# Attention in six float32 groups a unit: small float32 products moved next to the larger ones

## The reference

```python
q = xt @ Wq.T                                  # xt: x of a batch, turned; 8 heads of 32
scores = scale * einsum('bhqd,bhkd->bhqk', qh, qh)
logits = (scores * cmask + (1.0 - cmask) * NEG) * rmask
attn = softmax(logits, axis=-1)
ctx = einsum('bhqk,bhkd->bhqd', attn, qh)
out = ctx @ Wo.T                               # turned back, then the expert layers with a top-2 router
```

## Time and profile before

| what | us |
|---|---|
| median of 3 runs (1988.9 to 1992.98) | 1990.24 |
| the profiled execution | 2000.18 |
| its span, first to last instruction | 1998.4 |
| PE busy in the span | 1887.1 |

### The profile page before, as it was taken

The page is one execution under the profiler, slowest core; times in us unless marked ns, Lnnn a source line. Parts: engine busy times, 40 slices in busy tenths (PEclk is TensorE's granted clock), DMA queues, the critical chain, the costliest instruction groups (busy, mean ns, idle before and its releaser), DMA issues. The chain is left out here.

```text
span 1998.4 us, 27812 instructions
## 1 busy us (share of the span) xinstructions
PE 1887.1 (94%) x9512; PEld 1382.3 (69%) x9513; DVE 982.0 (49%) x1605; ACT 735.2 (37%) x1432; POOL 665.2 (33%) x500
## 2 busy tenths in 40 slices
PE   4999999999999859799999999989999999999999
PEld 2444444445444347698988999968788888888887
DVE  3677777777777438432333323245523233333333
ACT  1566667666666622343333433331001010101010
POOL 3576776767775616311111111111101001010100
PEclk7899999999999969999999999989999999999999
DMA  6786767676765063433333232253503021211111
GB/s 123 113 134 102 116 100 131 102 116 99 134 91 76 22 217 108 152 117 117 117 117 117 73 119 77 79 184 90 170 31 95 22 84 31 73 42 63 42 43 42
DMA packets 117636, 193.89 MB, mean 97 GB/s; under 512 B 11856, under 2 KB 43600, under 8 KB 117552
## 3 DMA queue, kind: packets, MB, share of 16 engines
q1 hardware_dynamic: 106912, 157.93, 35.3%
q0 software_dynamic: 10640, 34.87, 6.0%
HBM read 99.40 MB, written 42.21 MB: 71 GB/s over the span
## 5 line engine op out<-in xcount | busy, mean ns | idle before, releaser
L382 DVE TENSOR_REDUCE maxcol<-ps_m 128x1 f32<-128x512 f32 x512 | 342.5, 684 | 180.4 <-PE ps_m L525 173.4
L321 ACT ACTIVATE e<-ps_e 128x512 f32<-128x512 f32 x512 | 297.4, 596 | 191.1 <-PE ps_e L520 190.3
L126 POOL TENSOR_TENSOR e<-e 128x2048 f32<-128x2048 f32 x64 | 225.1, 3517 | 99.1 <-ACT e L321 99.1
L1416 ACT ACTIVATE s_silu<-s_ps_g 128x512 f32<-128x512 f32 x77 | 46.0, 598 | 560.9 <-PE s_ps_g L1539 560.9
L1384 POOL DMA_INDIRECT s_chosen<-routed,s_slot_now x64 | 63.4, 991 | 565.8 <-DVE s_total L1470 555.2
L520 PE MATMUL ps_e<-qside,kside 98*128 98x512 f32 x512 | 241.8, 475 | 9.2 <-ACT e L321 7.4
L1495 DVE TENSOR_TENSOR s_h_f<-s_silu,s_ps_u 128x512 f32<-128x512 f32 x77 | 53.0, 688 | 394.2 <-PE s_ps_u L1539 365.8
L520 PEld LDWEIGHTS ps_e<-qside,kside 98*128 98x128 f32 x512 | 96.4, 189 | 213.1 <-ACT e L321 175.4
L525 PE MATMUL ps_m<-kside,qside 97*128 97x512 f32 x512 | 215.3, 424 | 17.7 <-DMA qside<-row_mask 14.2
L1054 DVE TENSOR_TENSOR e_h_lo<-e_ps_h,e_h_hi 128x256 fp32r<-128x256 f32 (+1 forms) x136 | 41.9, 350 | 222.3 <-ACT e_h_hi L869 222.3
L1551 PE MATMUL s_ps_y<-s_d_hi,s_h_hi 128*128 128x512 f32 x352 | 137.8, 392 | 2.5 <-DVE s_h_lo L1452 1.9
(11 more groups left out here) (241 smaller groups left out, 3919.3 us busy)
## 6 DMA issues: line engine op xcount, KB each, us to landing
routed<-keep_y SPq DMA_DIRECT2D x68, 256.0 KB, 2.0
kside<-q_hi SPq DMA_DIRECT2D x64, 256.0 KB
qside<-qm_hi SPq DMA_DIRECT2D x64, 256.0 KB
x_f<-in_x SPq DMA_DIRECT2D x16, 512.0 KB, 4.0
kside<-q_lo SPq DMA_DIRECT2D x32, 256.0 KB
qside<-qm_lo SPq DMA_DIRECT2D x32, 256.0 KB
attn<-xo SPq DMA_DIRECT2D x32, 256.0 KB, 3.9
keep_rows<-attn SPq DMA_DIRECT2D x8, 1024.0 KB, 5.6
```

The costliest lines, as they stand in the source:

```text
L126: eng.tensor_tensor(into, into, e[k + 1][:, heads, :], ALU.add).then_inc(done, 1)
L321: act.activation(e[kb][:, g, :], ps_e[g % 2][:, :], ACT.Exp, scale=SCALE).then_inc(e_done, 1)
L382: dve.reduce_max(maxcol[par][:, g * KB + kb:g * KB + kb + 1], ps_m[g % 2][:, :], AX.X).then_inc(max_done, 1)
```

## The change

The number of products is the same. What changes is where they stand.

- PE: the turned values move from behind the first pair (`kb` 0) to behind the denominators at `kb` 1, for unit `u + 4` instead of `u + 3`, and so there are five value buffers instead of four. The projection moves from `kb` 2, `g` 0 to `kb` 0, `g` 3.
- The turned maxima move from `g` 2 to `g` 1, ahead of the numerators. The turned rows stand behind the numerators of `kb` 1, one half a unit; the partial logits behind the numerators of `kb` 2 and the logits behind the denominators of `kb` 3, in odd units. So float32 work stands in six places a unit.
- The output products of a batch `b` are made one half a unit at `kb` 2, `g` 3: half 0 in unit `2b + 3`, half 1 in unit `2b + 4`. Half 0 now waits for ACT's copy of the partial logits of the batch before it.
- ACT's copies move accordingly: q at `kb` 1, values at (2, 1), x high at (1, 2), turned rows at (1, 3), partial at (2, 2), output rows at (3, 0).
- POOL makes `x_lo` ahead of the sums of exponentials, not at the unit's end. SP stores one output half a unit.

```diff
-    v = [sb(f"v{n}", [P, KB, HG, DK], f32) for n in range(RING)]
+    VALUES = RING + 1
+    v = [sb(f"v{n}", [P, KB, HG, DK], f32) for n in range(VALUES)]
...
+    def batches(u):
+        odd = u % 2
+        return odd, (u - 4 - odd) // 2, (u - 4 + odd) // 2
...
@@ SP
-                if known(i, n, -3, hi=NU):
-                    for half in range(KT):
-                        b = 2 * i + (n - 3) // 2
...
+            half, b = 1 - n % 2, (u - 4 + n % 2) // 2
+            if 0 <= b < NB:
+                upto(sp, o_done, KT * b + half + 1)
...
@@ POOL
+            if n % 2 == 1 and known(i, n, 5):
...
+                pool.wait_ge(xhi_done, w + 1)
+                pool.tensor_tensor(x_lo[:], x_f[bp][:], x_hi[:], ALU.subtract).then_inc(x_split, 1)
             if known(i, n):
                 add_pair(pool, u, 0, slice(0, HG), pair_pool)
...
@@ PE
         def out_rows(u, b, half):
             upto(pe, c_split, UPB * (b + 1))
-            upto(pe, o_done, KT * b + half)
-            if known(i, n, 1):
-                pe.wait_ge(mt_done, RING * i + n + 2)
-            upto(pe, lg_done, b)
+            if u + 1 < NU:
+                pe.wait_ge(mt_done, u + 2)
+            if half:
+                pe.wait_ge(xt_done, KT * b + 1)
+            else:
+                upto(pe, partial_done, b)
+            upto(pe, lg_done, b - 1 + half)
...
+        def fp32_group(i, n, kb, before):
+            if kb == 0 and known(i, n, 1):
+                turn_maxima(i, n)
+            if before:
+                numerators(*before)
+            u = RING * i + n
+            odd, turned, projected = batches(u)
+            if kb == 1 and a_batch(turned):
+                turn_rows(u, turned, odd)
+            if kb == 2 and odd and a_batch(turned):
+                partial_logits(turned)
...
-                    if g == 0 and kb == 0 and known(i, n, 3):
-                        turn_values(i, n)
-                    if g == 0 and kb == 2 and known(i, n, 4):
+                    if g == 3 and kb == 0 and known(i, n, 4):
                         project(i, n)
-                    if g == 1 and before:
-                        numerators(*before)
...
+                    if g == 1:
+                        fp32_group(i, n, kb, before)
+                    if g == 3 and kb == 2 and a_batch(projected):
+                        out_rows(u, projected, 1 - odd)
+                    if g == 3 and kb == 1:
+                        if known(i, n, -1):
+                            denominators(u - 1, 1)
+                        if known(i, n, 4):
+                            turn_values(i, n)
+                    if g == 3 and kb == 3:
+                        if known(i, n):
+                            denominators(u, 0)
+                        if odd and a_batch(turned):
+                            logits(u, turned)
```

More of the change, by code:

```diff
@@ L323, in step @@
         def step(i, n):
-            even, odd = n % 2 == 0, n % 2 == 1
+            odd, turned, projected = batches(RING * i + n)
             if isinstance(i, int) and RING * i + n == 0:
@@ L389, in step @@
                         dve.reciprocal(den[par][:, c], den[par][:, c]).then_inc(over_done, 1)
-                if kb == 3 and n % 2 == 0 and known(i, n, -4, hi=NU):
-                    b = 2 * i + (n - 4) // 2
+                odd, b, _ = batches(u)
+                if kb == 3 and odd and a_batch(b):
                     dve.wait_ge(lg_mm, b + 1)
@@ L451, in turn_maxima, with turn_rows @@
         def turn_maxima(i, n):
-            upto(pe, max_done, (RING * i + n + 2) * KB * HG)
-            if n % 2 == 0:
-                upto(pe, o_done, KT * (2 * i + (n - 4) // 2 + 1))
-            else:
-                upto(pe, lg_done, 2 * i + (n - 5) // 2 + 1)
+            u = RING * i + n
+            odd, turned, projected = batches(u)
+            upto(pe, max_done, (u + 2) * KB * HG)
+            if odd:
+                upto(pe, o_done, KT * (turned + 1))
+            else:
+                upto(pe, o_done, KT * turned + 1)
+                upto(pe, lg_done, turned)
             nc.tensor.transpose(ps_o[0:HG * KB, 0:P], maxcol[(n + 1) % 2][:, :], ident[:, :]).then_inc(mt_mm, 1)
-        def turn_rows(i, n, half):
-            b = 2 * i + (n - 4) // 2
-            upto(pe, o_done, KT * (b + 1))
-            if half == 0 and known(i, n, 1):
-                pe.wait_ge(mt_done, RING * i + n + 2)
+        def turn_rows(u, b, half):
+            upto(pe, o_done, KT * b + half + 1)
+            upto(pe, lg_done, b)
+            if u + 1 < NU:
+                pe.wait_ge(mt_done, u + 2)
             upto(pe, xt_done, KT * b + half)
@@ L478, in partial_logits, with logits @@
             last.then_inc(partial_mm, 1)
-        def logits(i, n):
-            pe.wait_ge(partial_done, 2 * i + (n - 4) // 2 + 1)
+        def logits(u, b):
+            pe.wait_ge(partial_done, b + 1)
+            if a_batch(b + 1):
+                pe.wait_ge(o_done, KT * (b + 1) + 1)
             for half in range(KT):
```

89 lines of the change are left out of this document (36 added, 53 removed).

## The result

| kernel | median, us (lowest to highest) | ratio to before, 95% interval |
|---|---|---|
| before, beside it | 1991.61 (1988.9 to 1995.88) | |
| changed | 1962.07 (1959.41 to 1964.14) | 0.9845 (0.983 to 0.986) |
| changed, measured again | 1964.34 (1963.78 to 1968.99) | 0.9859 (0.9838 to 0.9881) |

The change makes the kernel about 29.5 us faster. The forecast was 1953 (37.5 us faster), so the sign and the main mechanism hold and the size was a quarter too large. The profiled execution of the changed kernel took 1962.56, almost the 1962.7 of the forecast's own sum.

The account below looks back on a forecast made before the run. PE, busy 94%, bounds the kernel. Per batch 2.33 + 0.78 - 0.43 = 2.68 us, with the other units and ends 37.5; 1962.7 against the profiled time, 1953 from the median; range 1937 to 1971.

Parts of the forecast that it names:

- The three old waits: PE waits behind turned maxima (1.36 us), at partial logits (0.62) and between output halves (0.35) go: 2.33 us a batch.
- a wait for ACT: Behind the turned maxima, PE waits 0.68 us a unit for ACT, busy with two copies while four pairs pass.
- Merging: Moving PE's small float32 products behind or ahead of tiled groups saves 0.78 us a batch.
- first rival: Merged transposes on PE save nothing, only the partial logits do: 2.10 us a batch, 1960 us; chance 0.22.
- The new wait: First output half of an odd unit waits on PE for ACT's copy of the partial logits: 0.43 us a batch added.
- PE starts 0.05 later: At the first output half in odd units, PE starts 0.05 us after ACT's copy of the partial logits ends.
- The third rival: The stack's DMA reaches PE too late, 1.6 us to spare; at 5 us late, about 2000 us; chance 0.06.
- 13 such batches: Units 2 to 27 of the attention stage each gain 2.68 us a batch, 34.8 us in all.
- The signs of being wrong: Batch over 39 us, PE waiting for stack or row of maxima, or over 10 us of difference behind attention.
- The ramp: At the start, projection and q come two row blocks earlier: 1.0 us saved, between 0 and 3.
- Units 28 and 29: No projection left, so four pairs stand together and the wait behind the maxima stays: 1.3 us saved.
- Units 30 and 31: Last units of the attention stage, only scores: 0.5 us saved.

Follow-up runs that it names:

- small groups apart: Changed kernel with turned maxima, turned halves, turned values and logits alone between pairs again, partial logits still behind the numerators; 1968.4 us, ratio 0.9863.
- the two experiments that take the wait away: Two kernels, each the changed kernel with one edit: x loaded behind the stack (1957.07 us), x low last (1960.88 us).
- all three: Changed kernel with x_lo last on POOL, partial logits copied before the exponential of (2, 2), and x loaded behind the stack on SP; 1950.65 us, ratio 0.9787.
- x low last, partial earlier: Changed kernel with POOL making x_lo at the odd unit's end and ACT copying the partial logits before the exponential of (2, 2); 1946.12 us, ratio 0.9775.
- partial copied earlier: Changed kernel with ACT copying the partial logits ahead of the exponential of (2, 2), not after it; 1957.33 us, ratio 0.9816.
- x loaded behind the stack: Changed kernel with SP issuing the load of x in the even unit, behind the stack and row of maxima; 1957.07 us, ratio 0.9825.
- x low last: Changed kernel with POOL making x_lo at the end of the odd unit, as the kernel before did; 1960.88 us, ratio 0.9835.

## Why the prediction was right, and where it was off

**The three old waits: right.** All of the 2.33 us are gone, each at its place: with the two terms below, 2.33 + 0.50 - 0.71 = 2.12 of the 2.13 us measured. The reason for the first was only partly right. The step "a wait for ACT, ... and has its context copy and the copy of the maxima in between" is at most 0.17 of 0.68 by the experiments; the larger part comes with four pairs in a row wherever they stand, from DVE in part. The forecast was safe from this, because the change leaves at most two pairs together.

**Merging: the mis-sized term.** The forecast had 0.78 us a batch, the rows give 0.50. A turned half or turned values behind a tiled group cost 0.41 + 0.32 - 0.34 = 0.39 where they cost 0.43 alone: 0.04 saved and not 0.10, four times. The maxima and the logits save nothing. The partial logits save 0.34 and not 0.20: they start 0.88 behind the numerators, where the forecast had 1.00 (the step to a score product). The Trainium skill, TensorEngine Tiling (Array Packing), section Tiling Modes, has the engine drain when the tiling mode changes. The rows agree: a tiled group behind a tiled one saves its entry, and a full-width transpose behind a tiled one saves next to nothing. The prediction gave that rule to its first rival, yet priced the one group that profits too low. (It says that the partial logits save a switch "twice a batch"; they stand once a batch, and its sum counts them once.) That rival, with transposes that save nothing, had 2.10 us a batch and 1960 in all, nearer to the measured 2.13 and 1962 than the forecast. Its rule is borne out but for the 0.04, and its number is in part luck: it has the partial logits 0.14 too low and the new wait 0.28 too low, and leaves out the four times 0.04.

**The new wait: right in place, too small.** 0.43 forecast, (0.86 + 0.31) - 2 x 0.23 = 0.71 measured. ACT was no later than thought: its copy ends 1.41 us behind the score product at 516.35, where the forecast had 1.41 as well.

```profile
517.38 0.38 ACT L310 ACTIVATE partial<-ps_o 128x256 f32<-128x256 f32 x1
```

The step that failed is "PE starts 0.05 later". The output half starts 0.25 behind the copy's end at 517.76, and the product behind it another 0.08 late. Nearly half of the wait is in what PE takes to start again, not in ACT.

The full width of the product is not the reason. In the trace of before, 26 score products of full width wait for ACT between 100 and 600 us, and each starts 0.05 behind the exponential that releases it. One is at 506.39, behind this one on ACT:

```profile
505.74 0.59 ACT L321 ACTIVATE e<-ps_e 128x512 f32<-128x512 f32 x1
```

What differs is how many wait instructions stand between the release and the product. The score products and the partial logits of before have none: their own weight load waits, and both start after 0.05, the forecast's number. The output half asks for several semaphores in a row (`out_rows`). Behind the copy's end two wait instructions pass, 0.11 apart, at 517.8 and 517.9 (`--source L109`), and only then comes the weight load. That is so at eleven of the twelve waits between 100 and 630 us. At the first output half of batch 0, where no earlier logits are asked for, there is one such instruction, and PE starts 0.15 behind the copy (171.92 + 0.38):

```profile
517.98 0.19 PEld L412 LDWEIGHTS ps_o<-c_hi,wo_hi 128*128 128x128 f32 x1 [0.87 <-issue]
```

```profile
172.45 0.47 PE L412 MATMUL ps_o<-c_hi,wo_hi 128*128 128x512 f32 x1 [0.36 <-ACT partial L310]
```

With small groups apart there is one as well ahead of each transpose that waits for DVE, and it too starts after 0.15. So 0.05, 0.15 and 0.25 go with none, one and two wait instructions. No experiment took them away.

These two terms, 0.28 and 0.28, are the whole difference between the forecast of 37.7 us a batch and the 38.27 measured, and 6.6 us over twelve batches.

**The transfer: a rival that half came true.** The third rival gave the stack 1.6 us to spare in a steady odd unit. There it holds nearly always, though with less: where PE does not wait for it, the row lands 0.5 to 1.2 us before PE needs it (3.2 to 5.3 in the kernel before), and four short waits cost 2.1 us over twelve batches. It was not counted for unit 3, whose neighbour unit 2 has no output half and no turned rows yet and takes 17.8 us, and where the row of maxima is issued behind both the load of x and the stack. The prediction took batch 1 as one of "13 such batches" at 2.68 us and got a loss of 2.74. That 5.4 us is the largest single miss of the first pair; in the second it is 2.2. In the traces of the two experiments that take the wait away, units 2 and 3 gain 3.1 and 2.6 us against the kernel before, as forecast.

**The signs of being wrong.** The prediction named three, and two came true. PE waited for the row of maxima, for 5.1 us in all. And 13 us of the first pair's difference lay behind the attention stage. That second sign tells of the spread of the expert stage and not of the change: in the second pair attention gave 28.8 us where the whole difference was 24.5.

**Smaller terms.** The ramp is not settled: 1.04 us in the first pair and 3.22 in the second, and among the changed kernel and its variants the first score product starts anywhere from 61.3 to 63.8. Units 28 and 29 were right, and for the reason given: with no projection, four pairs stand together, and from 601.87 to 605.41 the changed kernel has the same stall.

```profile
601.87 1.06 PE L423 MATMUL ps_num<-e,v 128*32 128x512 f32 x8
...
605.41 1.06 PE L423 MATMUL ps_num<-e,v 128*32 128x512 f32 x8
```

That is 3.54 us where 3.04 would do. Units 30 and 31 gained 3.04 us in place of 0.5, in both pairs. Part of it is the clock: in both traces of before some 3.4 us of them ran at a granted clock of 0.50 (665.6 to 669.0 in the first), and in both of the changed kernel none did. What such a stretch costs, two variants that should be alike there show: these units took 29.61 with one (all three) and 28.16 without (x low last, partial earlier). That is about 1.5 of the 3.04; the rest stays open. The tail cost 2.16 in place of 1.5 in the first pair and 4.78 in the second, so it can't be checked against the forecast: the changed kernel's took 28.48 both times, but that of before 26.32 and 23.70, with a granted clock of 0.50 and of 1.00 from 709.6 to 716.3.

**Why the total still came out near.** Attention gave 24.6 us in the first pair of traces and 28.8 in the second, where 37.5 were forecast. The first pair's miss of 13 is 6.6 for the steady terms and 7.5 for late transfers, less 1.1 for all the rest; the second pair gave 3.3 us more in units 2 and 3 and 3.5 more up to unit 2, and 2.6 less in the tail. Against the medians the forecast missed by 9.4 us. The profiled executions agreed only because the expert stage took 10.3 us more in the first trace of before than in the changed kernel's.

## What to carry to other kernels

Put small tiled float32 groups right behind other tiled ones; for full-width transposes the place made 0.04 us or nothing here, as long as what they wait for is done. Where a product has to start at once behind another engine, look at how many wait instructions stand ahead of it. Keep products that two other engines must drain in runs of no more than the banks there are, and place the large groups between them. And when waits go, count again what the shorter period asks of the DMA queue, the first short units apart from the steady ones: here one wait of 0.7 us a batch paid in full only together with an edit that issued the transfers earlier. By the medians the two gave 16 us together, and 1 and 5 alone, where neither stands clear of noise.

## What the runs showed that was not expected

A wait of PE can cost more than its length. In the last us of the 3.21 without work that end at 118.78, the granted clock fell to the lower of its two levels, 1.2 GHz (0.50), and it stayed there past 124 us. The windows of the changed kernel (stretch, us, busy time of PE, PEld, DVE, ACT and POOL with their instructions, granted clock, DMA share, GB/s):

```profile
98.00:114.00 16.00, 15.65 (x82) 7.41 (x82) 12.85 (x20) 11.24 (x22) 14.29 (x9) 1.00 0.81 135
...
118.00:120.00 2.00, 1.22 (x3) 1.03 (x4) 0.00 (x0) 0.33 (x1) 2.00 (x2) 0.50 1.06 132
120.00:124.00 4.00, 4.00 (x15) 1.42 (x14) 1.38 (x2) 1.96 (x5) 1.67 (x2) 0.50 1.10 136
124.00:126.00 2.00, 2.00 (x9) 1.63 (x8) 1.38 (x2) 1.38 (x3) 0.00 (x0) 0.85 1.11 139
126.00:138.00 12.00, 12.00 (x67) 6.24 (x66) 10.06 (x15) 9.60 (x17) 7.74 (x3) 1.00 0.13 18
```

Products 0.23 us apart at the full clock are 0.43 apart there (119.37 to 119.80). With the wait removed, units 2 and 3 are 5.85 us shorter, so about 2.6 us of it went to the clock: unit 3 took 20.54 where it takes 17.9. It does not happen each time. When the changed kernel was profiled again, PE stood 2.55 us at the same place, the clock stayed at its upper level (1.00), and unit 3 took 17.91:

```profile
114.00:116.00 2.00, 0.00 (x0) 0.00 (x0) 0.62 (x1) 0.00 (x0) 1.30 (x2) 1.00 0.92 170
118.00:124.00 6.00, 6.00 (x34) 3.56 (x34) 4.00 (x7) 4.74 (x10) 1.59 (x2) 1.00 1.08 131
```

The other two kernels that wait there agree with one or the other: 3.28 us, 0.50 and a unit 3 of 20.88 with the partial copied earlier, 2.47 us, 1.00 and 17.99 with small groups apart. So part of the spread between runs of the changed kernel can come from here, and x loaded behind the stack or x low last takes it away.

The windows also show how busy the DMA engines were while the row of maxima was on its way: a share of 0.81 to 1.11 in those shown up to 126 us, and 0.13 behind them.
